# Attention on eight cores: the row-sum matmuls of a key block are issued one score fill later on TensorE

## The reference

```python
scores = jnp.einsum('neax,nebx->neab', Q, K)
A = jax.nn.softmax(scores, axis=2)
Out = jnp.einsum('neab,neax->neax', A, V)   # = V * sum over b of A[a, b]
```

## Time and profile before

| what | us |
|---|---|
| median of 11 runs | 8512.18 |
| the profiled execution (slowest core) | 8525.08 |
| its span, first to last instruction, core 1 | 8523.5 |
| spans of the eight cores | 8489.0 to 8523.5 |
| stage B on core 1, first to last exponential | 5565.6 |
| busy in the span: PE / DVE / ACT | 4916.1 / 5402.7 / 4405.3 |

### The profile page before, as it was taken

One profiled execution on the slowest core, in us unless ns is written; L12 is line 12 of the kernel. 1 busy time (PEld: TensorE's weight loads), 2 busy tenths in 40 slices (PEclk: granted clock), 3 DMA queues, 4 the chain that ended last, 5 costly groups with the idle time before them and its releaser, 6 DMA issues. The chain is left out here.

```text
span 8523.5 us, 69885 instructions; the slowest of 8 cores (8489.0 to 8523.5 us)
## 1 busy us (share of the span) xinstructions
PE 4916.1 (58%) x24072; PEld 1504.4 (18%) x24072; DVE 5402.7 (63%) x4272; ACT 4405.3 (52%) x4868; POOL 151.2 (2%) x144
## 2 busy tenths in 40 slices
PE   4665555555555555555555555555523348777777
PEld 2221111111111111111111111111101113333322
DVE  4666677767777777767777777767746653222232
ACT  0007777777777777777777777777710000000000
POOL 0000000000000000000000000000000000000000
PEclk8876666666666666666666666666656568888887
DMA  3110000000000000000000000000042334455564
GB/s 70 40 36 4 1 0 1 1 1 1 0 1 1 1 0 1 1 1 1 1 1 1 1 1 1 1 1 1 1 83 68 88 69 65 65 74 74 75 83 60
DMA packets 348262, 206.26 MB, mean 24 GB/s; under 512 B 303840, under 2 KB 320224, under 8 KB 346864
## 3 DMA queue, kind: packets, MB, share of 16 engines
q0 software_dynamic: 273920, 92.70, 9.8%
q1 hardware_dynamic: 74000, 109.10, 4.4%
HBM read 235.75 MB, written 50.33 MB: 34 GB/s over the span
## 5 line engine op out<-in xcount | busy, mean ns | idle before, releaser
L417 PE MATMUL ps_sl<-qt,kt 64*128 64x512 bf16 x4096 | 1756.2, 522 | 2456.3 <-ACT eA L459 2114.8
L480 DVE TENSOR_SCALAR_CACHE_REDUCE eA<-eA 128x8192 bf16<-128x8192 bf16 x224 | 1945.7, 8686 | 1200.1 <-ACT eB L459 1200.1
L459 ACT ACTIVATE eA<-ps_sl,epsb 128x1024 bf16<-128x1024 f32 x1792 | 2000.4, 1116 | 1099.0 <-PE ps_sl L423 1099.0
L459 ACT ACTIVATE eB<-ps_sl,epsb 128x1024 bf16<-128x1024 f32 x1792 | 1993.1, 1112 | 0.0
L484 DVE TENSOR_SCALAR_CACHE_REDUCE eB<-eB 128x8192 bf16<-128x8192 bf16 x224 | 1944.6, 8681 | 0.0
L423 PE MATMUL ps_sl<-qt,kt 64*128 64x512 bf16 x4096 | 1794.9, 532 | 0.0
L390 PE MATMUL rps<-eA,lhsTall 128*16 128x512 bf16 x4096 | 1339.7, 499 | 30.6 <-DVE lhsTall L496 30.6
L396 PE MATMUL rps<-eB,lhsTall 128*16 128x512 bf16 x4096 | 1339.7, 499 | 0.0
L417 PEld LDWEIGHTS ps_sl<-qt,kt 64*128 64x128 bf16 x4096 | 268.5, 97 | 3835.0 <-issue 3835.0
L1053 ACT ACTIVATE s4lv<-s4vr,epsb 128x1 f32<-128x1 f32 x32 | 9.4, 294 | 1339.0 <-DVE s4vr L1137 1339.0
L390 PEld LDWEIGHTS rps<-eA,lhsTall 128*16 128x16 bf16 x4096 | 432.4, 110 | 1005.0 <-issue 816.4
(11 more groups left out here) (123 smaller groups left out, 3038.1 us busy)
## 6 DMA issues: line engine op xcount, KB each, us to landing
wotb<-wot POOLq DMA_DIRECT2D x64, 1024.0 KB, 11.1
xb<-x SPq DMA_DIRECT2D x64, 512.0 KB, 4.1
x1buf<-x1b SPq DMA_DIRECT2D x32, 512.0 KB, 5.2
x1b<-x1buf SPq DMA_DIRECT2D x32, 512.0 KB, 4.1
y<-yb SPq DMA_DIRECT2D x32, 512.0 KB, 4.9
vsp<-vt_tmp POOLq DMA_DIRECT2D x64, 128.0 KB, 2.1
vt<-vsp SPq DMA_DIRECT2D x8, 1024.0 KB, 7.7
wit_s<-wit POOLq DMA_DIRECT2D x1, 8192.0 KB, 71.6
```

The source lines that it names most:

```text
L417: mms.append(tensor.matmul(ps_sl[:, slA, half * 512:(half + 1) * 512], lhsA, qt[0:64, p, a0:a0 + 512], start=True, stop=True, tile_positio ...
L459: I(scalar.activation(ebuf[:, par, s2 * 1024:(s2 + 1) * 1024], ps_sl[:, sl, :], AF.Exp, scale=float(2.0 ** -10), bias=epsb[:, 1:2]), "s_exp")
L480: I(vector.tensor_scalar(eA[:, par, :], eA[:, par, :], 1.0, 0.0, ALU.mult, ALU.add, accum_out=cA[:, 0:1]), "s_dv")
```

## The change

`emit_R(K - 1)` behind the 8 fills of iteration K goes. In its place `emit_R(K - 2)` stands behind the first fill of iteration K, ahead of the second. R(K) so stands between the first and the second fill of iteration K+2, and no longer between the last fill of K+1 and the first of K+2. Behind the loop the two that remain, R(254) and R(255), are issued. The argument `skip_group_check` adds no instruction. No instruction is added or removed on any engine, the waits keep their numbers, and ACT, DVE, SP and POOL have the same rows as before.

```diff
@@ -392,18 +392,22 @@
                                 stop=(k == 63 and j == 15),
+                                skip_group_check=True,
                                 tile_position=(0, 0))
...
                     for K in range(NK):
                         p, k = K // 64, K % 64
                         for s2 in range(8):
+                            if s2 == 1:
+                                emit_R(K - 2)
                             gsA = K * 16 + 2 * s2
...
                             I(mms[3], "s_fill")
-                        emit_R(K - 1)
+                    emit_R(NK - 2)
                     emit_R(NK - 1)
```

## The result

The changed kernel takes 9051.67 us (median of 9 runs, 9048.35 to 9088.51) against 8512.18 before: ratio 1.0638, 95% interval 1.0621 to 1.0656. It is slower, by some 540 us; the forecast was 9005, range 8930 to 9075.

The account below looks back on a forecast made before the run. Stage B was taken as bound by ScalarE's 16 exponentials plus the uncovered part of R and one fill; 254 boundaries x 1.95 = 495 us on 8525.1 makes 9020, about 9005 after the profiled execution's 13 us excess; range 8930 to 9075.

Parts of the forecast that it names:

- R starts behind the sixteenth exponential: Stage B boundary: R starts 0.10 us after the sixteenth exponential's end, where it started 2.26 us before.
- ScalarE waits for R and not for a fill: Start of a stage B iteration: a matmul of R releases ScalarE's first exponential; gap 5.64 us, loss 1.95 per boundary.
- From R's end to ScalarE's start: Last term of the new gap: 0.09 us, as a fill's end shows.
- R's length: Term of the new gap: R taken as 5.45 us, somewhat above the mean of 5.23.
- ScalarE's own stretch: Between boundaries: raised clock may speed a third pair, nothing to -0.35 us per iteration, taken as nothing.
- VectorE, the end of a head pair, the other stages: VectorE's sums fit the longer iteration, its pair-end waits cost nothing more, stages A, C and D are untouched: nothing.
- R's wait for the weights: R's wait on `lhsTall` for VectorE's weights, 30.6 us, vanishes; it is already counted in the old gaps.
- the first (a clock low through R): Rival: in stage B R takes 6.9 us, gap 7.1; 4.1 per boundary, +1041, about 9555 us; chance 0.04.
- the second (a short R): Rival: every R in stage B takes 4.59 us, gap 4.78; +1.09 per boundary, +277, about 8790 us; chance 0.07.
- The fourth: Rival: ScalarE does not need R(K-2) at its start, only R's `lhsTall` wait goes; -31, about 8480 us; chance 0.03.
- The third: Rival: clock high when R starts, R 3.7 us, gap 3.9, slow pairs speed up; -394, about 8120 us; chance 0.03.
- The rule weighed: Skill's rule on TensorE: short pauses between matmul groups swing the clock and lose throughput; would speak for a worse outcome.

Follow-up runs that it names:

- the first run: Changed kernel, TensorE order untouched, R counts `s_rmm` eight times and ScalarE waits only for the part it needs: 8511.7 us, 0.9982 of the kernel before.
- the added matmuls: Changed kernel plus six unread matmuls behind each fill and six behind R: 8046.91, 8050.31, 8250.12 and 8608.88 us; no ratio given.

## Why the prediction was right

The mechanism held at each step, and the first run shows it by taking away the one wait that it names.

- *R starts behind the sixteenth exponential.* 0.10 us foretold, 0.11 in the rows.
- *ScalarE waits for R and not for a fill.* So it does at all 254 boundaries: 223 times before line 463 and 31 times before line 455, 1291.9 and 183.7 us, 5.81 each (5.64 foretold):

```profile
ACT eA L463 <- PE rps L397: 1291.9, 223, 6.0
ACT eA L455 <- PE rps L397: 183.7, 31, 5.9
```

- *From R's end to ScalarE's start.* This is the term that was mis-sized: 0.09, taken from a fill's end, was 0.22 (3092.43 to 3092.65), and 0.13 x 254 = 33 of the missing 47 us (9051.67 - 9005). That a last matmul that counts a semaphore is the same in both cases was a guess without a row. Why R's end takes longer to reach ScalarE no run here tells.
- *R's length.* 5.45 taken, 5.49 measured: 10 us. The lean towards a longer R was right; that it came so near was luck in part, as the rows before could not say when the clock would rise. It still rises inside R:

```profile
3085.00:3090.86 5.86, 4.99 (x24) 1.55 (x26) 3.94 (x1) 1.73 (x2) 0.00 (x0) 0.50 0.01 3
3090.86:3097.69 6.83, 2.79 (x22) 0.74 (x18) 6.83 (x3) 5.04 (x6) 0.00 (x0) 1.00 0.00 0
```

It rises 4.02 us after R's start here, and the iterations around this one are alike (23.88 from 3092.65 to 3116.53, the gap 5.92 at both ends), where three lengths took turns before.
- *ScalarE's own stretch.* Taken at nothing, and so it is: 23.88 - 5.92 = 17.96 us of the iteration above, as 21.36 - 3.40 before. One reading on the way to it was off, and nothing hangs on it: the second fill comes 1.47 behind R's end, where the next fill behind ScalarE's start came 3029.49 - 3027.60 = 1.89 before, so 0.42 sooner and not 0.65; by the prediction's own terms, 0.09 + 1.26, it would have been 0.54.
- *VectorE, the end of a head pair, the other stages.* Taken at nothing. Stage B accounts for 541.7 of the 540 us between the medians, so nothing is left for the other stages, and the gaps alone for (5.81 - 3.69) x 254 = 538, so little for the rest.
- *R's wait for the weights.* It shrank to 16.2 us, which is one wait, ahead of the last R of the stage, that nothing covers.

Of the rivals, the first (a clock low through R) and the second (a short R) didn't come: 0.64 in stage B and 5.49. The fourth, that the wait of ScalarE would not bind, is what the finer wait brings about by hand: the time is then that of the kernel before, still not less. The third was far off at the clock of this kernel, but the added matmuls show its side: with R at 930.3 / 256 = 3.6 us the changed order took 8046.91 and 8050.31 us, where that rival gave 8120. The rule weighed, that pauses make the clock swing at a cost, agrees with the swing in the rows, but its worse outcome did not come.

## What to carry to other kernels

Before moving a block of work later on one engine, look for who waits for its end: with two buffers the consumer of block K-2 must be done before the producer of K starts, and a block of the consumer that is issued so late that the producer has nothing left to do beside it is exposed whole. A wait that is small in the trace (30.6 us here) is no reason to give up an overlap that is large (2.26 us at the boundary shown, and 254 such boundaries). Where a long block stands between short steps of another engine, cut both the block and the wait for it: 2.13 us per iteration came back with a finer count alone, and a further 2.8 with the pieces spread between the steps.

## What the runs showed of the hardware

TensorE was busy for 7409.0 of 7411.8 us with fills, pieces of R and added 64-row matmuls, and the granted clock stayed at 0.50 throughout; with as many 128-row matmuls in their place it was 0.95. The Trainium skill ("TensorE: Matmul & The Clock Gate", section "Why this matters for your kernels") advises keeping TensorE busy without a break to reach the higher clock. The second run agrees with that; in the first TensorE was busy and the clock stayed low. The kind of matmul does not decide alone: in the changed order, with R in one block, the same 64-row matmuls behind the fills and behind R went with a clock of 0.99. Why these streams differ no run here tells. And work added for nobody made the kernel before faster: 8247.03 us with 10752 more matmuls (256 x 7 x 6), ratio 0.9635, at 0.95 of the clock in stage B where it had 0.66.
